# A scale table read straight from the input: one 2-row broadcast load a unit in place of eight copies in DRAM

## The reference, cut to what matters

```python
q_emb = relu(cond @ W3 + b3)
z = relu(((n * x + sum_n x) * q_emb) @ W2 + b2)
def dequant4bit(q, scale):                 # one scale for 64 neighbouring columns
    return (q.astype(float32) - 7.5) * repeat(scale, 64, axis=1)
y1 = z @ dequant4bit(w_up_q, w_up_scale).T + b_up + z @ up_a @ up_b
y2 = relu(y1) @ dequant4bit(w_down_q, w_down_scale).T + b_down + relu(y1) @ down_a @ down_b
out = x + y2
```

## Time and profile before

| | us |
|---|---|
| median of three runs | 765.12 |
| the profiled execution, its own time | 765.55 |
| its span on the core | 763.7 |
| TensorE busy | 740.0 (97%) |
| VectorE busy | 554.5 (73%) |
| ScalarE busy | 420.4 (55%) |
| GpSimd busy | 78.3 (10%) |

### The profile page before, as it was taken

One profiled execution on the slowest core, in us unless ns is written; L12 is line 12 of the kernel. 1 busy time (PEld: TensorE's weight loads), 2 busy tenths in 40 slices (PEclk: granted clock), 3 DMA queues, 4 the chain that ended last, 5 costly groups with the idle time before them and its releaser, 6 DMA issues. The chain is left out here.

```text
span 763.7 us, 9568 instructions
## 1 busy us (share of the span) xinstructions
PE 740.0 (97%) x3248; PEld 609.5 (80%) x3248; DVE 554.5 (73%) x725; ACT 420.4 (55%) x727; POOL 78.3 (10%) x68
## 2 busy tenths in 40 slices
PE   6599999999999999999999999999999999999997
PEld 5478888878878878888888888888888888888876
DVE  6598866776976487767776877767776877757585
ACT  3866175574754175666647265666656363626531
POOL 0063524333430000000000000000000000000000
PEclk9899999999999999999999999999999999999999
DMA  8957978988628696655516798766515696665552
GB/s 325 308 185 218 292 214 264 288 262 250 221 99 290 210 383 230 220 194 193 180 56 229 254 385 265 222 202 192 180 56 183 229 382 220 199 192 194 193 165 111
DMA packets 92160, 170.60 MB, mean 223 GB/s; under 512 B 8528, under 2 KB 25040, under 8 KB 91472
## 3 DMA queue, kind: packets, MB, share of 16 engines
q1 hardware_dynamic: 91824, 169.90, 67.4%
q10 hardware_dynamic: 288, 0.08, 0.0%
HBM read 130.10 MB, written 40.89 MB: 224 GB/s over the span
## 5 line engine op out<-in xcount | busy, mean ns | idle before, releaser
L1138 PE MATMUL ps<-x_hi,ring 128*128 128x512 f32 x672 | 262.1, 390 | 3.0 <-DVE x_lo L932 1.8
L1139 PE MATMUL ps<-x_lo,ring 128*128 128x512 f32 x672 | 261.5, 389 | 0.0
L1140 PE MATMUL ps<-x_hi,ring 128*128 128x512 f32 x672 | 261.4, 389 | 0.0
L1138 PEld LDWEIGHTS ps<-x_hi,ring 128*128 128x128 f32 x672 | 126.1, 188 | 31.4 <-DVE x_lo L932 2.7
L1140 PEld LDWEIGHTS ps<-x_hi,ring 128*128 128x128 f32 x672 | 126.1, 188 | 26.3
L1139 PEld LDWEIGHTS ps<-x_lo,ring 128*128 128x128 f32 x672 | 126.1, 188 | 26.1
L388 ACT ACTIVATE xt<-xt,gated,gate_n 128x64 f32<-128x64 f32 x216 | 74.6, 430 | 37.2 <-DVE gated L741 37.2
L497 ACT ACTIVATE f<-ps,bias 128x512 f32<-128x512 f32 x96 | 64.8, 690 | 42.2 <-PE ps L1140 42.2
L932 DVE TENSOR_TENSOR x_lo<-x_sum,x_hi 128x512 fp32r<-128x512 f32 x96 | 76.8, 818 | 4.2 <-ACT x_hi L535 3.4
L853 DVE TENSOR_TENSOR ps<-s,ps 128x512 f32<-128x512 f32 x48 | 33.3, 693 | 51.1 <-PE ps L1140 50.7
L890 DVE TENSOR_TENSOR res<-ps,res 128x512 f32<-128x512 f32 x72 | 48.3, 687 | 23.6 <-PE ps L1140 23.2
(11 more groups left out here) (80 smaller groups left out, 1002.0 us busy)
## 6 DMA issues: line engine op xcount, KB each, us to landing
ring<-made_w SPq DMA_DIRECT2D x336, 256.0 KB, 3.7
made_w<-made SPq DMA_DIRECT2D x16, 1280.0 KB, 6.0
xt<-in_x SPq DMA_DIRECT2D x32, 256.0 KB, 5.6
code<-in_codes SPq DMA_DIRECT2D x16, 512.0 KB, 8.3
scale<-made_s SPq DMA_DIRECT2D x16, 512.0 KB, 8.0
res<-in_x SPq DMA_DIRECT2D x4, 2048.0 KB, 10.1
made_w<-plain SPq DMA_DIRECT2D x64, 128.0 KB, 6.3
out<-res SPq DMA_DIRECT2D x12, 512.0 KB, 5.5
```

The costliest lines, as they stand in the source:

```text
L1138: pe.matmul(dest, w_hi, a_hi, start=start, stop=False, skip_group_check=True)
L1139: pe.matmul(dest, w_hi, a_lo, start=False, stop=False, skip_group_check=True)
L1140: return pe.matmul(dest, w_lo, a_hi, start=False, stop=stop, skip_group_check=True)
```

## The change

The tensor `made_s`, the DMA that fills it, its semaphore and the wait for it go. `load_scale` reads the two rows of its unit from the input and gives each to 64 partitions. The destination, its 512 KB and the row size of 4 KB stay.

```diff
-        COPIES = 8
-        made_s = nc.dram_tensor("made_s", [UNITS, 2, COPIES, 1024], F32, kind="Internal").ap()
-        scales_copied = sem("scales_copied")
             def load_scale(u):
                 if u >= 3:
                     sp.wait_ge(dequantized, u - 3 + 1)
-                rows = made_s[uid(FIRST[u])].rearrange("h c v -> (h c) v").unsqueeze(1)
-                sp.dma_start(scale[u % 3][:], rows.to_broadcast([2 * COPIES, P // 2 // COPIES, 1024])).then_inc(scale_loaded[u % 3], 16)
+                rows = scales[uid(FIRST[u])].unsqueeze(1)
+                sp.dma_start(scale[u % 3][:], rows.to_broadcast([2, P // 2, 1024])).then_inc(scale_loaded[u % 3], 16)
             for k in range(KD):
                 load_x(0, k)
                 sp.dma_start(raw_w2[:, k, :], w2[:, k, :]).then_inc(w2_raw[k], 16)
-                if k == 1:
-                    sp.dma_start(made_s, scales.unsqueeze(2).to_broadcast([UNITS, 2, COPIES, 1024])).then_inc(scales_copied, 16)
             sp.dma_start(raw_tables[:], tables[:]).then_inc(tables_loaded, 16)
             load_x(0, KD)
             load_x(0, KD + 1)
             load_codes(0)
-            sp.wait_ge(scales_copied, 16)
             load_scale(0)
```

## The result

| | before | after |
|---|---|---|
| median us (lowest to highest) | 765.16 (764.54 to 765.32) | 842.93 (841.84 to 844.01) |
| profiled execution | 765.55 | 842.03 |
| span | 763.7 | 840.2 |
| low half of plain, unit 3, starts at | 74.98 | 105.47 |
| the same, unit 13 | 192.96 | 270.95 |

The changed kernel is slower by a ratio of 1.1006 (95% interval 1.0987 to 1.1026), 77.8 us. The forecast was 858 us in 835 to 905: direction, place and mechanism came out, and the forecast was 15 us too large.

A forecast was written before the change was run, and what follows sets the result against it. TensorE was taken to bound the kernel, until two DMA engines bind the changed loop. A shift of 84.4 us, 1.7 for the clock and 6.6 for disturbed rates make 92.7 on 765.55: 858 us, range 835 to 905.

The forecast's parts named there:

- Two engines, cut along the outermost count: Scale loads: source outermost count 2 confines each to 2 DMA engines, 64 rows each; near the undisturbed rate, chance 0.70.
- A share of 10.2 us: Each scale load: 262,144 B on each of two engines at 25.8 GB/s takes 10.2 us, where 8 rows took 1.3 to 1.8.
- The sum: Transfers worked off in order on one of two engines: 17.6 us a unit, TensorE starts unit 13 at 283.4, +84.4 us.
- The allowance for disturbed rates: Loop transfers: a tenth of the way to fully disturbed rates, 0.6 us in each of 11 units, 6.6 us.
- The last pause's clock loss: TensorE after its last loop pause: a lowered granted clock costs 1.7 us.
- The signs: Loop: DMA share about a half, units of 17 to 19 us, TensorE waiting for plain's low half every unit, later work only shifted.
- A queue that is never empty: Loop's DMA queue: 17 us of work still stands when made u goes out, so it stays fed, by some 6 us.
- Spread as before: Rival for scale loads: divided by destination rows, only the removal counts, 763 us; chance 0.07 faster, 0.03 the same.
- slow rows: Rival for scale loads: 16 engines read the same 8 KB slowly; at three times the read time 783 us; chance 0.04.
- Well disturbed: Rival for the loop: two engines at disturbed rates, 23.4 us a unit, 937 us, halfway 894; chance 0.12.
- A clock that stays low: Rival for TensorE's loop: granted clock 0.50 for whole units, 60 us more, 918 us; chance 0.04.
- The removal: At the start, without the DRAM copy and SP's wait, x parts come sooner: 0 to 3.2 us gained.

The follow-up runs named there:

- the old order: SP's loop as in the kernel before (765.16 us): loads of scale u+4 and codes u+3 issued ahead of the plain stores of unit u.
- the dose of 1, 2, 4 and 8 copies: Kernel before with 1, 2 or 4 copies of the scales in DRAM in place of its 8: 845.95, 786.14 and 770.68 us.
- the new order: Plain stores issued ahead of scale and codes loads from u = 1: changed kernel 845.57 us, two copies 772.19, four copies 764.47, two halves 761.93.
- 4 and 8 engines: Kernel before with two copies of the scales in DRAM (4 engines a scale load), 786.14 us, and with four copies (8 engines), 770.68 us.
- the two halves: Changed kernel with each scale load issued as two DMAs, one row to 64 partitions each, 16 engines, no copies: 760.54 us, ratio 0.9933.
- the kernel with one copy: Kernel before with one copy of the scales in DRAM in place of eight, the copy and its wait kept: 845.95 us, ratio 1.1055.

## Why the prediction was right, point by point

**What bounded the kernel.** That TensorE bounds the loop held: where 16 engines share the loads in the old order, the unit stays at 11.66 to 11.80 us. How little the DMA engines have to spare was the number to watch.

**Two engines, cut along the outermost count.** Shown, by the small packets, by the DMA share of 0.13 and by the dose of 1, 2, 4 and 8 copies. The trace of before had no row for this; the number of small packets would have been the way to read it from any kernel with an odd pattern.

**A share of 10.2 us.** Shown: 0.13 share at 52 to 53 GB/s.

**The sum.** Its first mark, the low half of unit 2's weights, came by its own steps at 87.5 + 1.6 + 1.05 = 90.1; measured 89.53. The loop was mis-sized: 17.45 us a unit on average (192.0 from there to unit 13's low half at 282.1), measured 181.4, 16.5 a unit. The terms at fault are the two stores, whose rates came from windows of before in which other transfers mixed with them. The made store was put at 333 GB/s, 3.9 us a share; by the 402 GB/s above it is 3.3, and eleven of them are 7.4 us less. The plain stores were put at 339 GB/s, 1.55 us; no row has them alone, but at 25.8 GB/s an engine they are 1.27, and eleven are 3.0 us less. That is 10.4 of the 10.6 us, and the bytes of the eleven units over 181.4 us are 25.6 GB/s an engine. So the undisturbed rate, read from one kind of transfer, held for all of them.

TensorE was to start unit 13 84.4 us late and was 73.7. The allowance for disturbed rates (6.6 us) was for nothing: with 14 engines idle half the time, the two run as in an undisturbed stretch. The last pause's clock loss (1.7) did not show at unit 13: the granted clock from 272 to 281 us is 1.00. And one wait was missing from the sum: the low-rank product in the middle of unit 13 comes 2.9 us later than the matmuls ahead of it allow (2.78 of idle time in the row above), for the weights of unit 14. 73.7 + 2.9 = 76.6 us, the measured shift. The errors had both signs: with the missing wait in the sum the forecast would have been 861 us, so a little of the closeness is luck.

The top of the range was added up wrongly: a third of the way from 858 to the fully disturbed 937 is 884, not 905. The measured time lies inside either way.

**The signs.** A DMA share of about a half (0.54) and a shift that nothing behind unit 13 changes were right. Units of 17 to 19 us were not: 16.5. Nor did TensorE wait for the low half of plain in every unit: three times, and most often for the low-rank product.

**A queue that is never empty.** Right for two engines: the new order gave nothing back, and the bytes fill their time. But the same ring of waits that I had checked only for emptiness becomes the bound in the middle, at 4 and 8 engines. It runs over two units: from the low half of unit u+1 to the made store of u, 9.7 us (before: 146.42 to 156.14); then, on the fullest engine, made 3.3, scale, codes 1.3, plain 1.5; landing and cast 2.7. That is 18.5 us plus the scale's share, so 10 us a unit with 1.3, 10.5 with 2.5 and 11.8 with 5.1 at undisturbed rates: near TensorE's 11.8 already, and these loads run disturbed. These sums are estimates and fall short of the measured 12.36 and 13.20; what is shown is that taking the loads out of the ring brings the unit back.

**The rivals.** "Spread as before" and "slow rows" are refuted by the packets and by the two halves. "Well disturbed" is refuted by 26 GB/s an engine. "A clock that stays low": over seven units the mean granted clock is 0.90, so TensorE is at the lower of its two levels for part of the loop, and it is busy for 12.86 us of the unit shown where it was 11.7. From 89.53 to 270.95 us this makes 17 of the 22.2 us of extra busy time. It still waited in that unit, so the low clock filled part of a pause that the queue made anyway, and did not become the bound. No run has two engines at a full clock, so this is argued from the idle time and from the two full engines.

**The removal.** 0 to 3.2 us, said the sum; with two halves it is 3.0 us at the pause that it named, 4.9 at the end. In the changed kernel that early gain was lost: scale 0 stood ahead of x 6 and 7, for which VectorE waited until 28.96 us (26.98 before). Against the kernel with one copy, which has the wait and the two engines, the changed one is 2.7 us better (77.8 us lost, not 80.5); of that no more than 0.8 is there at unit 3, and the rest is in its units, 16.55 against 16.66 us.

## What to carry to other kernels

Before a broadcast load is written, look at the outermost count of both of its patterns, and give it one that 16 divides. Here that was done by splitting the transfer in two, without copies in memory. When a DMA is slow, read the DMA share against the GB/s (0.13 at 53 GB/s is two full engines) and count the small packets. And place stores that release a buffer ahead of loads that are early anyway: a queue in order is part of every ring of waits that passes through it, and here it cost time (5 us with 8 engines a load) before its engines were full.

## What the runs showed of the hardware that was not expected

Issuing itself was slow where two engines had fallen behind. SP's issue of two x parts took 6.46 us behind the first two-row load and that of the four w2 stores 14.05 us, where it was 1.12 and 1.76 (the rows below the second dots):

```profile
7.26 0.68 SPq L279 DMA_DIRECT2D scale<-in_scales  x1
7.98 6.46 SPq L267 DMA_DIRECT2D xt<-in_x  x2
...
28.69 14.05 SPq L333 DMA_DIRECT2D made_w<-w_ring  x4
...
12.90 1.12 SPq L270 DMA_DIRECT2D xt<-in_x  x2
...
19.32 1.76 SPq L339 DMA_DIRECT2D made_w<-w_ring  x4
```

So in these rows the delay stands as issue time of the next DMA, of 128 to 512 KB, and not as a wait; that a full queue is what holds the issue is inferred. And one engine moved no more than its sixteenth part of the full rate: 26 GB/s, with fourteen others idle.
